# A fused attention and mixture layer on eight cores: the reciprocals of each head's softmax sums move ahead of the next head's first tiles on VectorE

## The reference

```python
q = (x @ Wq + bq).reshape(B, S, H, Dh)        # 16 heads of 64
k = (x @ Wk + bk).reshape(B, S, H, Dh)
v = (x @ Wv + bv).reshape(B, S, H, Dh)
r = (x @ Wr + br).reshape(B, S, H, Dr)        # 32 more per head
q = jnp.concatenate([q, r], axis=-1)
k = jnp.concatenate([k, r], axis=-1)
scores = jnp.einsum('bqhd,bkhd->bhqk', q * scale, k)
attn = jax.nn.softmax(scores, axis=-1)
out = jnp.einsum('bhqk,bkhd->bqhd', attn, v).reshape(B, S, H * Dh)
return out @ Wo + bo
```

## Time and profile before

| | us |
|---|---|
| median of the two timed executions | 7271.22 |
| the two timed executions | 6817.39 and 7725.05 |
| profiled execution, its own time | 6774.98 |
| profiled execution, span of the slowest core | 6773.3 |
| PE busy in the span | 5662.2 (84%) |
| DVE busy in the span | 3200.8 (47%) |
| ACT busy in the span | 1645.6 (24%) |

### The profile page before, as it was taken

The page is one execution under the profiler, slowest core; times in us unless marked ns, Lnnn a source line. Parts: engine busy times, 40 slices in busy tenths (PEclk is TensorE's granted clock), DMA queues, the critical chain, the costliest instruction groups (busy, mean ns, idle before and its releaser), DMA issues. The chain is left out here.

```text
span 6773.3 us, 73438 instructions; the slowest of 8 cores (6760.7 to 6773.3 us)
## 1 busy us (share of the span) xinstructions
PE 5662.2 (84%) x25267; PEld 2591.8 (38%) x25512; DVE 3200.8 (47%) x4508; ACT 1645.6 (24%) x2639; POOL 361.6 (5%) x588
## 2 busy tenths in 40 slices
PE   4999996965889988888988888988686889959993
PEld 1444443422334433334433333443343334424441
DVE  2221212223777777777677777777553222222212
ACT  2222222222333333333333333333221010011100
POOL 1111111210000000000000000000000000010001
PEclk9999998977889988889988888998898899979996
DMA  3242243210000000000000000000122011021101
GB/s 103 47 76 57 48 76 69 64 32 38 20 11 16 17 21 21 21 11 16 16 21 21 21 12 16 16 20 1 47 83 71 28 56 50 32 81 53 53 25 47
DMA packets 70771, 259.94 MB, mean 38 GB/s; under 512 B 11266, under 2 KB 11394, under 8 KB 67282
## 3 DMA queue, kind: packets, MB, share of 16 engines
q0 software_dynamic: 43392, 140.81, 8.4%
q1 hardware_dynamic: 27026, 114.43, 5.2%
HBM read 183.24 MB, written 71.96 MB: 38 GB/s over the span
## 5 line engine op out<-in xcount | busy, mean ns | idle before, releaser
L725 ACT ACTIVATE p<-scp 128x1024 f32<-128x1024 f32 x1024 | 1047.9, 1023 | 2135.9 <-PE scp L707 2135.9
L707 PE MATMUL scp<-q,k 97*128 97x512 bf16 x6144 | 1414.9, 380 | 137.3 <-DMA v<-vscr 137.0
L682 PE MATMUL avp<-p2h,v 128*65 128x512 bf16 x4096 | 1321.8, 384 | 195.8 <-DVE at_l L661 191.6
L707 PEld LDWEIGHTS scp<-q,k 97*128 97x128 bf16 x6144 | 597.7, 98 | 866.3 <-issue 155.2
L1262 PE MATMUL epp<-ewh,at_h 128*128 128x512 bf16 x1995 | 763.5, 383 | 84.6 <-DVE acc L1285 82.4
L1262 PE MATMUL epp<-ewl,at_h 128*128 128x512 bf16 x2012 | 770.6, 383 | 35.3 <-DVE ewl L1217 30.2
L682 PE MATMUL avp<-p2l,v 128*65 128x512 bf16 x2048 | 787.5, 384 | 0.0
L1262 PE MATMUL epp<-ewh,at_l 128*128 128x512 bf16 x2012 | 769.8, 383 | 2.0 <-issue 0.2
L734 DVE CAST p2h<-p 128x1024 bf16<-128x1024 f32 x512 | 355.4, 694 | 847.9 <-ACT p L725 847.9
L682 PEld LDWEIGHTS avp<-p2h,v 128*65 128x65 bf16 x4096 | 462.0, 113 | 672.6 <-issue 250.2
L748 DVE TENSOR_TENSOR p2l<-p,p2h 128x1024 bf16<-128x1024 f32 x512 | 627.5, 1226 | 55.0 <-DVE p2h L743 1.8
(11 more groups left out here) (165 smaller groups left out, 4602.9 us busy)
## 6 DMA issues: line engine op xcount, KB each, us to landing
wst<-ew POOLq DMA_DIRECT2D x128, 512.0 KB, 3.7
k<-kscr SPq DMA_DIRECT2D x16, 1552.0 KB
v<-vscr SPq DMA_DIRECT2D x16, 1040.0 KB
xt<-x_kv SPq DMA_DIRECT2D x32, 512.0 KB, 18.2
kscr<-ev POOLq DMA_DIRECT2D x128, 128.0 KB, 2.7
q<-qscr SPq DMA_DIRECT2D x16, 776.0 KB
vscr<-vst_h POOLq DMA_DIRECT2D x8, 1040.0 KB, 18.6
vscr<-vst_l POOLq DMA_DIRECT2D x8, 1040.0 KB, 28.3
```

The source lines that it names most:

```text
L682: last = e.matmul(av_ps[qt][0:65, :], v2[pb][:, va * VL + kc * 65: va * VL + kc * 65 + 65], b[:, qt * 512:qt * 512 + 512], start=(kc == 0 ...
L707: last = e.matmul(sps[:, qi * 512:qi * 512 + 512], k2[pb][0:97, ka * S + kc * 128: ka * S + kc * 128 + 128], q2[pb][0:97, qa * SQ + qt * 5 ...
L725: lambda e: e.activation(p32[pp][:, half * 1024: half * 1024 + 1024], sps[:, :], AF.Exp, scale=SCALE))(),
```

## The change

The four reciprocals of `sched_evac` become a function of their own, `sched_evac_recips`. Inside the loop it is called at the start of head `hh`, ahead of everything of that head, for head `hh - 1`. The rest of the evacuation, `sched_evac`, stays where it was, at `kc == 1`. For the last head the two are called one behind the other, as before. Waits, semaphores, operands and the number of operations stay the same; only the place of the four reciprocals in DVE's queue changes, for 15 of 16 heads.

```diff
+                def sched_evac_recips(hh):
                     for qt in range(4):
                         p.add("vector",
                               (lambda qt=qt: lambda e: e.reciprocal(
                                   linv[64:65, qt * 512:qt * 512 + 512],
                                   av_ps[qt][64:65, :]))(),
                               waits=[(s2av, p.cur(s2av))], inc=s2li)
+
+                def sched_evac(hh):
+                    rows0 = (hh % 2) * 64
+                    chj = hh // 2
                     li_base = p.cur(s2li)
...
                 for hh in range(H):
                     pb = hh % 2
                     d2val = p.cur(s2d[pb])
+                    if hh > 0:
+                        sched_evac_recips(hh - 1)
                     if hh + 1 < H:
                         head_load(hh + 1)
...
                     if hh == H - 1:
+                        sched_evac_recips(hh)
                         sched_evac(hh)
```

More of the change, by code:

```diff
@@ L606, in head_load @@
                               waits=(wt if j == 0 else []), inc=s2d[pb])
-                def sched_evac(hh):
-                    rows0 = (hh % 2) * 64
-                    chj = hh // 2
+                def sched_evac_recips(hh):
                     for qt in range(4):
```

## The result

| us | before | after |
|---|---|---|
| median of all timed executions | 7140.63 (23) | 6833.53 (26) |
| shortest timed execution | 6769.04 | 6734.16 |
| profiled execution, its own time | 6774.98 | 6735.99 |
| span of the slowest core | 6773.3 | 6734.2 |
| ratio after / before, like with like | | 0.9942, interval 0.9929 to 0.9954 |

The ratio says 0.6% faster, 31 to 48 us by its interval; the profiled executions differ by 39.0 us, the shortest timed ones by 34.9. The forecast gain was 38.0, the forecast time 6737.0.

The account below looks back on a forecast made before the run. PE was taken to wait for DVE's run in 15 passages between heads; filling 2.53 us of DVE's idle time in each gives 38.0 us, so 6774.98 - 38.0 = 6737.0 us, with no change for the clock; range 6700 to 6815.

Parts of the forecast that it names:

- What bounds the kernel: Attention stage: PE bounds inside a head; in 15 passages between heads PE waits for DVE's run.
- When the reciprocals start: Between heads: 0.49 us after the last product's start, filling 2.53 of DVE's 4.24 us idle time.
- The delayed casts and the broadcasts: Between heads: casts' 10.5 us delay is covered by the evacuation; broadcasts finish 5.9 us before the first copy; no cost.
- The reciprocal's duration: First two reciprocals beside four exps: no change taken; 19% more on each would remove the gain.
- The restart: PE's products after each evacuation: restart at 1808.20 instead of 1810.73, 2.53 us earlier in each of 15 passages.
- TensorE's clock: Half-clock stretch behind each restart: no net change taken; bounds 25 us gain and 40 us loss.
- more than 5 us at half behind a restart: Behind PE's restart between heads: half clock for over 5 us was listed as a sign of a wrong prediction.
- the rival that the clock takes back half (19 us): Behind restarts: clock rises at the same moment as before, leaving 19 us gain, 6756; chance 0.22, shared with slowed reciprocals.
- The sum: Whole kernel: 15 x 2.53 = 38.0 us off the profiled 6774.98, giving 6737.0 us.
- How the numbers follow: Chances and ranges: gain of 28 to 48 us 0.62, half 0.22, nothing or small loss 0.07, more than 48 0.09.
- the upper end of the range: Whole time: 6817.39 less half the gain, 19, is 6798, raised to 6815 for little gain at that height.
- The range for the likeliest case: Whole time: 6727 to 6747 us around the forecast 6737; gain of 28 to 48 us, chance 0.62.

Follow-up runs that it names:

- the last experiment: Changed kernel, but all heads except the last copy av_ps to SBUF, take reciprocals on 128 x 16 elements, spread the evacuation over next-head tiles; 6253.29 to 6254.35 us.

## Why the prediction was right or wrong

- *What bounds the kernel.* Right. PE waits for DVE's run in 15 passages; leaving out 6.42 us of that run brought 95 to 104 us where 103 were due, and taking nearly all of it off the path brought 483.
- *When the reciprocals start.* Right: 0.48 us after the last product's start, forecast 0.49. The idle time ahead of the first cast, 4.24 us, shrank to the 1.71 ahead of the reciprocals. That it is this time and nothing else is shown by the experiment that fills none of it (no gain) and the one that fills it with a single reciprocal (nearly the whole gain).
- *The delayed casts and the broadcasts.* Right: both are covered. The last pair of broadcasts ended at 1788.7, 5.7 us before the copy that needs it (forecast 5.9).
- *The reciprocal's duration.* Right: 12.99 us for four beside exps, the bound of 19% more was not touched. What the Trainium skill states ("PSUM — Partial Sum Buffer", Specifications (TRN2)), that ScalarE and VectorE reach PSUM in parallel at full bandwidth unless they meet in one bank, agrees with this: the four exps beside the first two reciprocals also kept their 1.02 us.
- *The restart.* 2.64 us earlier instead of 2.53. The 0.11 us more are in DVE's run: from the start of the eight operations to that of the next one it was 7.86 us, now 7.74. 15 x 2.64 = 39.6 us.
- *TensorE's clock.* I took no change, with bounds of 25 us gain and 40 us loss. It costs 5 us. I had also named more than 5 us at half behind a restart as a sign that the prediction is wrong, and 5 of the 15 passages of core 1 have it (5.8 to 6.1 us): my zero for the clock was wrong in single passages and nearly right only as a mean. The windows view of the 8 us behind a restart shows it in the third column from the end (granted clock, then DMA share and GB/s). Passages 4 to 6 of the kernel before (core 0):

```profile
2415.99:2423.99 8.00, 8.00 (x30) 3.68 (x31) 0.83 (x2) 1.86 (x2) 0.00 (x0) 0.79 0.07 29
2617.22:2625.22 8.00, 8.00 (x29) 3.63 (x30) 0.76 (x2) 1.78 (x2) 0.00 (x0) 0.78 0.07 29
2818.73:2826.73 8.00, 8.00 (x30) 3.67 (x31) 0.81 (x2) 1.84 (x2) 0.00 (x0) 0.79 0.07 29
```

and the first three of the changed kernel (core 1):

```profile
1809.10:1817.10 8.00, 8.00 (x29) 3.64 (x30) 0.71 (x2) 1.74 (x2) 0.00 (x0) 0.77 0.06 27
2008.03:2016.03 8.00, 8.00 (x31) 3.72 (x32) 1.19 (x2) 2.05 (x2) 0.00 (x0) 0.83 0.06 26
2206.26:2214.26 8.00, 8.00 (x24) 3.36 (x25) 0.00 (x0) 0.93 (x1) 0.00 (x0) 0.64 0.06 27
```

  A mean clock of 0.79 over 8 us is 3.4 us at half; 0.77, 0.83 and 0.64 are 3.7, 2.7 and 5.8 us. In the kernel before the stretch starts at 4.5 us or more and settles near 3.4 from the fourth passage on; in the changed one it goes round among about 4, 3 and 6 us. The means over the 15 passages and all eight cores are 3.61 us before and 4.29 after, so 15 x 0.68 / 2 = 5.1 us are given back, and 39.6 - 5.1 = 34.5 us remain. The attention stage, measured as above over all eight cores, became 3226.4 - 3190.8 = 35.6 us shorter. So a mean of zero change was a little too kind, and the rival that the clock takes back half (19 us) was far off. The rule on long pauses that I weighed from the Trainium skill ("TensorE: Matmul & The Clock Gate", HAM oscillation) agrees with the traces in that each of these pauses is followed by a stretch at half clock. What lengthens the stretch is not the pause, as two experiments show. With the reciprocals behind tile 0 the pause is longer (16.6 us in passages 4 to 6) and the time from restart to restart as before (201.5 us), and the stretch stays near 3.4 (core 4):

```profile
2414.07:2422.07 8.00, 8.00 (x30) 3.65 (x31) 0.81 (x2) 1.83 (x2) 0.00 (x0) 0.78 0.06 27
2615.34:2623.34 8.00, 8.00 (x29) 3.64 (x30) 0.75 (x2) 1.77 (x2) 0.00 (x0) 0.78 0.07 29
```

  With only the first reciprocal early the pause is as before (12.67 to 12.98 us) and the time from restart to restart as in the changed kernel (199.5 us, there 199.1), and the stretch varies between 2.7 and 6.1, with a mean of 4.45 over all cores (below, the first two passages of core 2):

```profile
1802.98:1810.98 8.00, 8.00 (x28) 3.58 (x29) 0.65 (x1) 1.57 (x2) 0.00 (x0) 0.75 0.06 27
2002.40:2010.40 8.00, 8.00 (x24) 3.35 (x25) 0.00 (x0) 0.87 (x1) 0.00 (x0) 0.63 0.06 26
```

  So in these kernels the stretch changed with the time from restart to restart; why was not tried.
- *The sum.* 38.0 us forecast, 39.0 measured between the profiled executions, 31 to 48 by the ratio. The agreement is partly luck: the stage gave 35.6 us, and what is missing to 39 is scatter between cores and executions outside of it (the rest of the program after the stage takes 1939.5 us before and 1939.3 after, as a mean of the cores).
- *How the numbers follow: the step that failed.* The mechanism and its 38 us held; the step that failed is the upper end of the range, the term for the height of the timed execution. I made the forecast and the range for a time of the profiled execution's kind. I wrote that the median of 7271.22 was "no base", since its two executions lie 908 us apart, and then let the upper end reach only from the shorter of the two, 6817.39 less half the gain, to 6815. That allowed for a time at most 78 us above the forecast of 6737. But the time to be forecast was itself a median over all executions. 14 of the 26 took 6819 to 7688 us, so the median fell just among them, at 6833.53, 98 us above the profiled execution; in the kernel before it lay 366 us above. The 908 us between two executions were the measure of that uncertainty and stood in the table; a range for the median should have reached far above 7000 us. The range for the likeliest case, 6727 to 6747, held all 12 of the others (6734.16 to 6740.67). That the median came out as near to the range as it did is chance: with one more short execution in place of a long one it would have fallen inside it.

## What to carry to other kernels

Where one engine waits for another's unbroken run of work, only the length from the release to the end of that run counts: fill idle time at its head with whatever is ready, and one operation longer than the gap does it; moving more, or having work done earlier that lies beside, changes only who is said to wait. Then ask whether the run must lie on the path at all: here a copy of 2.48 us freed the buffers that 35 us of work had held, and was worth twelve times the reordering. When a time is forecast, look at what will be measured: where two executions of one kernel differ by 13%, the range must hold both, or say for which of them it speaks.

## What the runs showed of the hardware

- A reciprocal of 1 partition x 512 elements takes 3285 ns on DVE, one of 128 x 16 elements 246 ns in the last experiment, for the same 2048 results for which the four took 12.99 us. The long ones read PSUM and the short one SBUF, and no run separates that from the number of elements per partition.
- The stretch at half clock behind a pause is not a fixed cost. A steady 3.4 us became a round of 4, 3 and 6 us when the time from restart to restart changed by 1% (201.5 to 199.1 us), with the pause before it longer (20.40 us) or as before (12.67), so a small gain ahead of a restart can return as anything between -1.3 and +0.4 us of clock in one passage.
- Matmuls that are not used can hold the clock up through a pause: the granted clock was 0.88 over all 78 of the first passage, and behind the restart 1.00 there and in 101 of 120 passages.
